# A layer kernel's state sums reordered: the second chunk's sum ahead of the state products, and VectorE's block layouts around gate times up

## The chip, the cores and the metric

The kernel runs on one core of one Trainium2 chip. The metric is device time in microseconds, the median of three runs. The span of a profiled execution is the time from its first instruction to its last. TensorE (PE in the profile) does the matrix products and is the only engine that writes PSUM here; VectorE (DVE), ScalarE (ACT) and GpSimd (POOL) work element by element; SyncE's queue (SP) issues the transfers.

## The reference

A normalised input goes through two branches that are added to the input: causal linear attention with 16 heads of 16 channels, and a mixture of four small gated MLPs with a router, plus a short convolution.

```python
x  = L0_attn_x                       # (8, 2048, 256) float32
xn = _layernorm(x)
# attention: q, k = relu(xn @ wq), relu(xn @ wk); v = xn @ wv
kv  = jnp.cumsum(k[..., :, None] * v[..., None, :], axis=2)
num = jnp.einsum('bhnd,bhnde->bhne', q, kv)
den = jnp.einsum('bhnd,bhnd->bhn', q, jnp.cumsum(k, axis=2))[..., None] + EPS
attn = (num / den) @ wo
# experts: top 2 of 8; four are MLPs, the others copies of x or relu(x), or nothing
g, u = jnp.einsum('th,ehi->tei', xn, Wg), jnp.einsum('th,ehi->tei', xn, Wu)
hid  = silu(g) * u
ffn  = sum_e cw_e * (hid_e @ Wd_e) + cw_4 * x + cw_6 * x + cw_7 * relu(x) + conv(x)
out  = x + attn + ffn
```

## The kernel before

The 8 sequences of 2048 tokens are cut into 32 batches of 512 tokens (`BT`), four to a sequence, and a batch into four tiles of 128 tokens (t = 0 to 3). A tile is two chunks of 64 tokens; chunk n = 2t + h. The causal sum is not formed for each token: within a chunk a masked score matrix (`sm`) times the values gives what the chunk's own tokens contribute, and a running 16x16 state for each head, summed over all earlier chunks, is multiplied with the queries.

All engines run their own programs, written out by hand, and meet at counting semaphores. One batch on TensorE (`batch`, in the section `block.tensor`) is, for each tile t:

- `gate_up(t)`: twelve products of 128x128 weights with 512 columns, for expert t (line 300 with `wgu_h` and `wgu_l`), six for the gate and six for up. Each half waits until VectorE has read the PSUM bank it writes: the gate half for `s_gu` (hid of the tile before), the up half for `s_y` (yT of the tile before).
- `numerators(t)`: `state_sum(2t + 1)` (line 371), then the scores times values (line 408), then the state times query (line 422), which ends with `s_num`, and then `state_sum(2t + 2)` except for the last tile.
- after tile 0 the next scores (line 357), after tile 1 the transposes of the next batch's input (line 310).

After the four tiles come the next batch's projections (`heads`) and the outputs of this batch (`output`).

`state_sum(n)` adds the keys-times-values product of chunk n to a running sum that stays in one PSUM bank (`ST`, "state_sum" in the profile). Before it may add, VectorE must have read the sum of the chunks before: it waits on `s_bd` for `blocks(n)`. VectorE's `blocks(n)` (line 760) waits on `s_st` for `state_sum(n - 1)`, multiplies the bank with a mask, and writes the block-diagonal operand `state_bd[:, n % 4]` that the state times query of chunk n uses. So the sums and the layouts form a chain that alternates between the engines: sum 2t+1, layout 2t+2, sum 2t+2, layout 2t+3.

On VectorE a tile is `gate_up(t)` (line 783: hid = up times silu of gate, waits for the up half and for ScalarE's silu), then `attend(t)`: layout 2t+2, the numerators over the denominators (yT, line 796), layout 2t+3. Then come two convolution taps (line 775), or after tile 0 the masking of the next scores (line 753). ScalarE and GpSimd split hid and yT into high and low parts for later products; GpSimd also weighs hid (line 626).

In the profile a float32 matmul appears as two passes, so that `state_sum`'s 8 products are 16 rows of a MATMUL, the 32 scores-times-values products 64, and the 8 state-times-query products 16. Their array shapes (rows by columns of weights) differ: 64x32 for `state_sum` and for scores times values, 128x64 for state times query, 128x128 for gate and up and for the transposes and projections, 32x64 for scores.

Of the kernel before, what the change touches and what calls it, by code (L numbers as in the profile page):

```python
# [15 lines left out]
def layer_kernel(nc, x, wqkv, wo, w_router, router_bias, w_gate, w_up, w_down, conv_w, conv_b,  # L16
# [6 lines left out]
    T = 4  # L23
    BT = T * P
    BPS = seq_len // BT
# [19 lines left out]
    with ExitStack() as ctx:  # L45
# [247 lines left out]
        def _(pe):  # L293
# [67 lines left out]
            def state_sum(s, j, k, n):  # L361

                first = (j + k) % BPS == 0 and n == 0
                if not first:
                    pe.wait_ge(s_bd, chunk_at(s, j + k, n))
                t, h = n // 2, n % 2
                toks = slice(h * HALF, (h + 1) * HALF)
                for g in range(C):
                    for m in range(PPG):
                        rows = slice(BLK * m, BLK * m + BLK)  # L370
                        ins = mm(ST[rows, g, :], ktok[toks, t, g, rows], vp[toks, t, g * PPG + m, 0:3:2, :],  # L371
                                 start=first and g == 0, stop=True, skip_group_check=True)
                ins.then_inc(s_st, 1)

            def batch(s, j, left):
                last = left == 0
                p = j % 2

                def gate_up(t):
                    for u in range(2):  # L380
                        if t == 0:

                            pe.wait_ge(s_out, at(s, j, T, 2 + u))
                        else:

                            pe.wait_ge((s_gu, s_y)[u], at(s, j, T, t))
                        product((GB, UB)[u][t % 2], [(wgu_h[:, u, t, c, :], wgu_l[:, u, t, c, :], xh[:, p, c, :],
                                                     xl[:, p, c, :]) for c in range(C)]
                                ).then_inc((s_gp, s_up)[u], 1)

                def numerators(t):
                    first_tile = j == 0 and t == 0
                    if t == 0:
                        pe.wait_ge(s_out, at(s, j, T, T))
                    pe.wait_ge(s_sg, at(s, j, T, t + 1))
                    if j < BPS - 1 or t < T - 1:
                        state_sum(s, j, 0, 2 * t + 1)
                    if t % 2 == 0:
                        pe.wait_ge(s_sm, at(s, j, U * ROWS, ROWS * (t // 2 + 1)))
                    for g in range(C):  # L400
                        gs = slice(g * HALF, (g + 1) * HALF)
                        for par in range(2):
                            for m in range(PPG):
                                pair = g * PPG + m
                                for h in range(2):
                                    toks = slice(h * HALF, (h + 1) * HALF)
                                    window = vp[toks, t, pair, par:par + 2, :].rearrange("p a d -> p (a d)")
                                    mm(NB2[t % 2][h][BLK * m:BLK * m + BLK, gs], window,  # L408
                                       sm[toks, t // 2, t % 2, 2 * pair + par, :], start=par == 0 and g == 0,
                                       stop=False, skip_group_check=True)  # L410
                    for h in range(2):
                        if first_tile and h == 0:
                            continue
                        n = 2 * t + h
                        pe.wait_ge(s_bd, chunk_at(s, j, n))
                        for g in range(C):
                            n0 = t * P + h * HALF
                            for w in range(2):

                                rows = slice(w * HALF, (w + 1) * HALF)  # L420
                                cols = slice(g * P + w * HALF, g * P + (w + 1) * HALF)
                                ins = mm(NB2[t % 2][h][rows, g * HALF:(g + 1) * HALF], state_bd[:, n % 4, cols],  # L422
                                         qT[:, g, n0:n0 + HALF], start=False, stop=True, skip_group_check=True)
                    ins.then_inc(s_num, 1)
                    if t < T - 1:
                        state_sum(s, j, 0, 2 * t + 2)

                def output(t):
                    ts = slice(t * P, (t + 1) * P)
                    dst = OB[t]  # L430
                    if t == 3:
                        pe.wait_ge(s_out, at(s, j, T, T + 1))
                    elif t == 0 or last:
                        pe.wait_ge((s_y, s_gu, s_y)[t], at(s, j, T, T))
                    else:
                        pe.wait_ge(s_sig, at(s, j, T, T + 2 + t))
                    if t == 0:
                        pe.wait_ge(s_conv, at(s, j, HALO, HALO))
                    for c in range(C):
                        mm(dst[:, c * P:(c + 1) * P], cT[:, c, ts], ident_s[:, :], is_transpose=True,  # L440
                           start=c == 0, stop=False, skip_group_check=True)
                    pe.wait_ge(s_yl, at(s, j, T, t + 1))
                    product(dst[:, 0:D], [(yh[:, c, ts], yl[:, c, ts], wo_h[:, c, :], wo_l[:, c, :])
                                          for c in range(C)], first=False, final=False)
                    for e in range(E):
                        if t == 0:
                            pe.wait_ge(s_hl, at(s, j, T, e + 1))
                        ins = product(dst[:, 0:D], [(hh[:, e, ts], hl[:, e, ts], wd_h[:, e, :], wd_l[:, e, :])],
                                      first=False, final=e == E - 1)
                    ins.then_inc(s_op, 1)  # L450

                for t in range(T):
                    gate_up(t)
                    numerators(t)
                    if t == 0:
                        scores(s, j, 0, 1)
                    if t == 1 and not last:
                        for c in range(C):
                            turn_xn(s, j, 1, c)
                if not last:  # L460
                    heads(s, j, 1)
                for t in range(T):
                    if t == T - 1 and not last:
                        scores(s, j, 1, 0)
                        state_sum(s, j, 1, 0)
                    output(t)
# [200 lines left out]
        def _(dve):  # L667
# [89 lines left out]
            def blocks(s, j, k, n):  # L757

                dve.wait_ge(s_st, chunk_at(s, j + k, n))
                dve.tensor_tensor(state_bd[:, n % 4, :].rearrange("p (g m n) -> p g m n", g=C, m=PPG),  # L760
                                  ST.unsqueeze(2).to_broadcast([P, C, PPG, BLK]),
                                  same_head_s[:, :].rearrange("p (m n) -> p m n", m=PPG).unsqueeze(1)
                                  .to_broadcast([P, C, PPG, BLK]), ALU.mult).then_inc(s_bd, 1)

            def batch(s, j, left):
# [17 lines left out]
                    dve.tensor_tensor(hid[:, t, :], UB[t % 2], sg[:, :], ALU.mult).then_inc(s_gu, 1)  # L783

                def attend(t):
                    if t < T - 1:
                        blocks(s, j, 0, 2 * t + 2)
                    elif j < BPS - 1:
                        blocks(s, j, 1, 0)
                    dve.wait_ge(s_num, at(s, j, T, t + 1))  # L790
                    if t > 1:
                        dve.wait_ge(s_yl, at(s, j, T, t - 1))
                    if t == 0:
                        dve.wait_ge(s_rd, at(s, j, C, C))
                    r = t % 2
                    dve.tensor_tensor(yT[:, t % 2, :, :].rearrange("p g (h n) -> p g h n", h=2),  # L796
                                      ring[:, r:r + 2, 0:P].rearrange("p h (g n) -> p g h n", g=C),
                                      rdT[:, :, t * P:(t + 1) * P].rearrange("p g (h n) -> p g h n", h=2),
                                      ALU.mult).then_inc(s_y, 1)
                    if t < T - 1:  # L800
                        blocks(s, j, 0, 2 * t + 3)

                for t in range(T):
                    gate_up(t)
                    attend(t)
                    if t == 0:
                        mask(s, j, 0, 1)
                    else:
                        tap(t)
# [92 lines left out]
```

## Time and profile before

| | |
|---|---|
| median of 3 runs | 1348.21 us (1348.19 to 1348.37) |
| the profiled execution's own time | 1346.54 us |
| its span | 1344.8 us |
| granted TensorE clock, mean | 0.997 of full speed |
| PE busy | 1313.8 us, 98% of the span |
| DVE busy | 1114.9 us, 83% |
| POOL / ACT busy | 814.9 us, 61% / 738.3 us, 55% |

Busy time counts an engine's instructions, not its waits. The matmul ends are modelled by the profiler, so 98% says that TensorE always had something in flight, and not that it ran at its peak. The chain that ended last is followed back from the last instruction; the engine that carries it is the one whose own instruction stream sets the time.

### The profile page before, as it was taken

What the parts mean: (1) busy time and instruction counts of PE and PEld (TensorE: products, weight loads), DVE (VectorE), ACT (ScalarE), POOL (GpSimd) and SP (SyncE); (2) the same over time, 40 slices, a digit from 0 to 9 for tenths busy, and PEclk for the clock granted to TensorE, in tenths of its full rate; (3) what the DMA queues carried; (4) which work ended last, traced back from release to release, by engine and by line L of the source; (5) the groups of instructions that cost most, each with busy time, mean ns of one, the idle gap of its engine ahead of it and who ended that gap; (6) DMA issues with size and microseconds to landing.
All of it is one profiled execution on the core that took longest, in us unless ns stands there. A gap on an engine that the chain in (4) does not pass through costs nothing.

```text
span 1344.8 us, 54748 instructions
## 1 busy us (share of the span) xinstructions
PE 1313.8 (98%) x24384; PEld 1136.4 (85%) x24384; DVE 1114.9 (83%) x2566; ACT 738.3 (55%) x1545; POOL 814.9 (61%) x679
## 2 busy tenths in 40 slices
PE   4899999999999999999999999999999999999997
PEld 3788888888888888888888888888888888888886
DVE  4888888888888888988888988888888889888885
ACT  4555665555664565654555655555645656545561
POOL 2755666755666656657556666556566566575554
PEclk9999999999999999999999999999999999999999
DMA  4011111111111211111111111121111111111110
GB/s 148 34 66 65 51 48 34 65 65 66 46 53 34 65 65 64 35 45 55 66 65 51 48 35 65 65 65 42 56 35 66 65 65 35 34 65 50 50 49 18
DMA packets 46779, 73.73 MB, mean 55 GB/s; under 512 B 6480, under 2 KB 42192, under 8 KB 42448
## 3 DMA queue, kind: packets, MB, share of 16 engines
q1 hardware_dynamic: 46544, 70.24, 15.1%
q8 instruction: 191, 3.13, 1.0%
q14 instruction: 44, 0.36, 0.1%
HBM read 53.18 MB, written 17.04 MB: 52 GB/s over the span
## 4 chain that ended last, share of the span: by engine, by line
PE 97%; DVE 1%; SPq 1%; ACT 1%; DMA 1%; issue 0%; DVEq 0%
PE ring L300 51%; PE scores L300 17%; PE ring L408 7%; PE ring L422 6%; PE scores L357 5%; PE state_sum L371 4%; PE ring L440 2%; PE scores L310 2%; PE scores L339 2%; DMA x_t<-in_L_attn_x_dram 1%; SPq L257 0%; DVE cT L775 0%; ACT qp L517 0%; DVE sm L753 0%; ACT xn L528 0%
## 5 line engine op out<-in xcount | busy, mean ns | idle before, releaser
L626 POOL TENSOR_TENSOR hid<-hid,cwb 128x512 f32<-128x512 f32 x128 | 169.8, 1327 | 202.6 <-DVE hid L783 200.8
L775 DVE SCALAR_TENSOR_TENSOR cT<-xT,conv_ws,cT 128x512 f32<-128x512 f32 x192 | 288.8, 1543 | 0.0
L614 POOL TENSOR_TENSOR x_t<-x_t,same 128x1024 f32<-128x1024 f32 x32 | 77.1, 2409 | 264.3 <-ACT same L524 264.3
L540 ACT ACTIVATE sg<-ring 128x512 f32<-128x512 f32 x128 | 76.7, 599 | 281.5 <-PE ring L300 281.5
L300 PE MATMUL ring<-xl,wgu_h 128*128 128x512 f32 x512 | 212.0, 414 | 0.0
L300 PE MATMUL ring<-xh,wgu_l 128*128 128x512 f32 x512 | 202.5, 396 | 0.0
L300 PE MATMUL ring<-xh,wgu_h 128*128 128x512 f32 x512 | 201.8, 394 | 0.0
L630 POOL TENSOR_TENSOR hl<-hid,hh 128x512 fp32r<-128x512 f32 x128 | 193.2, 1509 | 0.0
L783 DVE TENSOR_TENSOR hid<-ring,sg 128x512 f32<-128x512 f32 x128 | 88.2, 689 | 110.9 <-PE ring L300 110.9
L480 ACT ACTIVATE yh<-yT 128x256 fp32r<-128x256 f32 x128 | 53.5, 418 | 228.9 <-DVE yT L796 228.9
L753 DVE TENSOR_TENSOR sm<-scores,causal_s 128x512 f32<-128x512 f32 x256 | 158.7, 681 | 20.4 <-PE scores L357 20.2
L300 PE MATMUL ring<-wd_h,hl 128*128 128x256 f32 x512 | 143.7, 281 | 0.0
L300 PE MATMUL ring<-wd_h,hh 128*128 128x256 f32 x512 | 143.4, 280 | 0.0
L300 PE MATMUL ring<-wd_l,hh 128*128 128x256 f32 x512 | 143.2, 280 | 0.0
L635 POOL TENSOR_TENSOR yl<-yT,yh 128x256 fp32r<-128x256 f32 x128 | 132.7, 1036 | 7.7 <-ACT yh L480 7.2
L408 PE MATMUL ring<-sm,vp 64*32 64x64 f32 x8192 | 118.9, 225 | 0.0
L300 PEld LDWEIGHTS ring<-xl,wgu_h 128*128 128x128 f32 x512 | 96.8, 189 | 23.7 <-issue 5.5
L300 PEld LDWEIGHTS ring<-xh,wgu_l 128*128 128x128 f32 x512 | 96.4, 188 | 22.6
L300 PEld LDWEIGHTS ring<-xh,wgu_h 128*128 128x128 f32 x512 | 97.0, 190 | 17.3
L371 PEld LDWEIGHTS state_sum<-vp,ktok 64*32 64x32 f32 x3968 | 54.1, 107 | 57.8 <-issue 51.2
L760 DVE TENSOR_TENSOR state_bd<-state_sum,tables_s 128x256 f32<-128x256 f32 x248 | 102.6, 414 | 0.0
L408 PEld LDWEIGHTS ring<-sm,vp 64*32 64x32 f32 x8192 | 98.2, 105 | 2.9 <-issue 2.9
(110 smaller groups left out, 3542.6 us busy)
## 6 DMA issues: line engine op xcount, KB each, us to landing
cwb<-cw_rows SPq DMA_DIRECT2D x32, 1024.0 KB, 4.6
x_t<-in_L_attn_x_dram SPq DMA_DIRECT2D x32, 512.0 KB, 4.4
out_dram<-x_t SPq DMA_DIRECT2D x32, 512.0 KB, 2.9
cw_rows<-cwt SPq DMA_DIRECT2D x128, 2.0 KB, 1.4
sm<-in_L_attn_wqkv_dram SPq DMA_DIRECT2D x2, 384.0 KB, 5.5
sm<-in_L_ffn_Wg_dram SPq DMA_DIRECT2D x2, 256.0 KB, 4.2
sm<-in_L_ffn_Wu_dram SPq DMA_DIRECT2D x2, 256.0 KB, 5.8
cwb<-in_L_ffn_Wd_dram SPq DMA_DIRECT2D x1, 512.0 KB, 4.2
```

Source lines behind the costliest of these rows:

```text
L300: ins = mm(dst, lhs, rhs, start=first and n == 0, stop=final and n == len(passes) - 1, skip_group_check=not first)
L371: ins = mm(ST[rows, g, :], ktok[toks, t, g, rows], vp[toks, t, g * PPG + m, 0:3:2, :], start=first and g == 0, stop=True, skip_group_check ...
L408: mm(NB2[t % 2][h][BLK * m:BLK * m + BLK, gs], window, sm[toks, t // 2, t % 2, 2 * pair + par, :], start=par == 0 and g == 0, stop=False, ...
L422: ins = mm(NB2[t % 2][h][rows, g * HALF:(g + 1) * HALF], state_bd[:, n % 4, cols], qT[:, g, n0:n0 + HALF], start=False, stop=True, skip_gr ...
L614: pool.tensor_tensor(xb, xb, same[:, :, :], ALU.add).then_inc(s_base1, 1)
L626: pool.tensor_tensor(hid[:, e, :], hid[:, e, :], cwb[:, e, :], ALU.mult).then_inc(s_hid, 1)
L630: pool.tensor_tensor(hl[:, e, :], hid[:, e, :], hh[:, e, :].bitcast(F32), ALU.subtract).then_inc(s_hl, 1)
L635: pool.tensor_tensor(yl[:, :, t * P:(t + 1) * P], yT[:, t % 2, :, :], yh[:, :, t * P:(t + 1) * P].bitcast(F32), ALU.subtract).then_inc(s_y ...
L753: dve.tensor_tensor(heads, SB[f][:, :].rearrange("p (t a n) -> p t a n", a=2, n=HALF), causal2_s[:, :].unsqueeze(1).unsqueeze(1).to_broadc ...
L760: dve.tensor_tensor(state_bd[:, n % 4, :].rearrange("p (g m n) -> p g m n", g=C, m=PPG), ST.unsqueeze(2).to_broadcast([P, C, PPG, BLK]), s ...
L775: ins = dve.scalar_tensor_tensor(out=cT[:, c, :], in0=xT[:, j % 2, c, n:n + BT], scalar=conv_ws[:, c, n:n + 1], in1=cT[:, c, :], op0=ALU.m ...
L783: dve.tensor_tensor(hid[:, t, :], UB[t % 2], sg[:, :], ALU.mult).then_inc(s_gu, 1)
```

## The change

TensorE: the second state sum of a tile, `state_sum(2t + 2)`, is moved ahead of the state times query. VectorE: `blocks(2t + 2)` (for the last tile `blocks` of the next batch) is moved ahead of gate times up, and `blocks(2t + 3)` from behind yT to ahead of it.

```diff
@@ TensorE, numerators(t): after scores times values
+                    if t < T - 1:
+                        state_sum(s, j, 0, 2 * t + 2)
                     for h in range(2):
                         ...
                                 ins = mm(NB2[t % 2][h][rows, g * HALF:(g + 1) * HALF], state_bd[:, n % 4, cols],
                                          qT[:, g, n0:n0 + HALF], start=False, stop=True, skip_group_check=True)
                     ins.then_inc(s_num, 1)
-                    if t < T - 1:
-                        state_sum(s, j, 0, 2 * t + 2)
@@ VectorE
                 def attend(t):
-                    if t < T - 1:
-                        blocks(s, j, 0, 2 * t + 2)
-                    elif j < BPS - 1:
-                        blocks(s, j, 1, 0)
                     dve.wait_ge(s_num, at(s, j, T, t + 1))
                     ...
                                       ALU.mult).then_inc(s_y, 1)
+
+                for t in range(T):
+                    if t < T - 1:
+                        blocks(s, j, 0, 2 * t + 2)
+                    elif j < BPS - 1:
+                        blocks(s, j, 1, 0)
+                    gate_up(t)
                     if t < T - 1:
                         blocks(s, j, 0, 2 * t + 3)
-
-                for t in range(T):
-                    gate_up(t)
                     attend(t)
```

No instruction is added or removed. On TensorE, tile 1 of the first batch, before; `state_sum` is the running sum, `ring<-sm,vp` scores times values, `ring<-qT,state_bd` state times query:

```order
L371 MATMUL state_sum<-vp,ktok 32x32 [waits s_bd,s_sg]
L371 MATMUL state_sum<-vp,ktok 32x32 x7
L408 MATMUL ring<-sm,vp 32x64 x32
L422 MATMUL ring<-qT,state_bd 64x64 [waits s_bd]
L422 MATMUL ring<-qT,state_bd 64x64 x3
L422 MATMUL ring<-qT,state_bd 64x64 [waits s_bd]
L422 MATMUL ring<-qT,state_bd 64x64 x3
L371 MATMUL state_sum<-vp,ktok 32x32 [waits s_bd]
L371 MATMUL state_sum<-vp,ktok 32x32 x7
L310 MATMUL scores<-tables_s,xn 128x128 [waits s_sm,s_xn]
```

The same place in the changed kernel:

```order
L371 MATMUL state_sum<-vp,ktok 32x32 [waits s_bd,s_sg]
L371 MATMUL state_sum<-vp,ktok 32x32 x7
L408 MATMUL ring<-sm,vp 32x64 x32
L371 MATMUL state_sum<-vp,ktok 32x32 [waits s_bd]
L371 MATMUL state_sum<-vp,ktok 32x32 x7
L424 MATMUL ring<-qT,state_bd 64x64 [waits s_bd]
L424 MATMUL ring<-qT,state_bd 64x64 x3
L424 MATMUL ring<-qT,state_bd 64x64 [waits s_bd]
L424 MATMUL ring<-qT,state_bd 64x64 x3
L310 MATMUL scores<-tables_s,xn 128x128 [waits s_sm,s_xn]
```

The second sum stands right behind the products that have its array shape, and its wait for VectorE's layout now comes ahead of the state times query instead of behind it. On VectorE the same tile, before, from hid to the first tap:

```order
L783 TENSOR_TENSOR hid<-ring,sg 128x512 [waits s_up,s_sg]
L760 TENSOR_TENSOR state_bd<-state_sum,tables_s 128x256 [waits s_st]
L796 TENSOR_TENSOR yT<-ring,qks 128x256 [waits s_num]
L760 TENSOR_TENSOR state_bd<-state_sum,tables_s 128x256 [waits s_st]
L775 SCALAR_TENSOR_TENSOR cT<-xT,conv_ws,cT 128x512 [waits s_tap0]
```

And in the changed kernel:

```order
L760 TENSOR_TENSOR state_bd<-state_sum,tables_s 128x256 [waits s_st]
L783 TENSOR_TENSOR hid<-ring,sg 128x512 [waits s_up,s_sg]
L760 TENSOR_TENSOR state_bd<-state_sum,tables_s 128x256 [waits s_st]
L792 TENSOR_TENSOR yT<-ring,qks 128x256 [waits s_num]
L775 SCALAR_TENSOR_TENSOR cT<-xT,conv_ws,cT 128x512 [waits s_tap0]
```

Both layouts (L760) have moved one instruction forward: the first past hid, the second past yT. The TensorE move is made in the tiles 0, 1 and 2 of each of the 32 batches, 96 places; the VectorE move of the first layout also in tile 3, except in the last batch of a sequence.

## Rows read from the trace of the kernel before

**Rows 1.** The page: busy shares, and the chain that ended last.

```profile
PE 1313.8 (98%) x24384; PEld 1136.4 (85%) x24384; DVE 1114.9 (83%) x2566; ACT 738.3 (55%) x1545; POOL 814.9 (61%) x679
...
PE 97%; DVE 1%; SPq 1%; ACT 1%; DMA 1%; issue 0%; DVEq 0%
```

**Rows 2.** Waits of PE: who was waited for, us in total, times, longest.

```profile
PE scores L310 <- POOL xn L600: 10.0, 1, 10.0
PE scores L300 <- DVE wqk_l L833: 9.2, 1, 9.2
PE ring L440 <- DVE cT L775: 3.4, 1, 3.4
PE scores L357 <- ACT ktok L480: 2.3, 1, 2.3
PE state_sum L371 <- DVE state_bd L760: 2.2, 1, 2.2
```

**Rows 3.** Timeline of PE, a tile 2: start us, us, engine, line, op, out<-in.

```profile
626.04 0.40 PE L300 MATMUL ring<-xh,wgu_l 128*128 128x512 f32 x1
626.37 0.25 PE L371 MATMUL state_sum<-vp,ktok 64*32 64x32 f32 x5
...
626.50 0.19 PE L371 MATMUL state_sum<-vp,ktok 64*32 64x32 f32 x1
626.52 0.84 PE L408 MATMUL ring<-sm,vp 64*32 64x64 f32 x59
627.28 0.69 PE L422 MATMUL ring<-qT,state_bd 128*64 128x64 f32 x16
627.90 0.33 PE L371 MATMUL state_sum<-vp,ktok 64*32 64x32 f32 x16
628.16 0.51 PE L300 MATMUL ring<-xl,wgu_h 128*128 128x512 f32 x1
```

**Rows 4.** Durations of the lines 371, 422 and 760, min/median/max ns.

```profile
L371 PE MATMUL state_sum<-vp,ktok x3968: 186/193/260, 36.3 to 1321.9; 64*32 64x32 f32 x199
```

```profile
L422 PE MATMUL ring<-qT,state_bd x1984: 222/222/271, 44.0 to 1326.3; 128*64 128x64 f32 x199
```

```profile
L760 DVE TENSOR_TENSOR state_bd<-state_sum,tables_s x248: 405/415/425, 42.5 to 1322.2; 128x256 f32<-128x256 f32 x124
```

**Rows 5.** Timeline of PE, the tile 3 that follows.

```profile
632.05 0.69 PE L422 MATMUL ring<-qT,state_bd 128*64 128x64 f32 x16
632.67 0.39 PE L300 MATMUL scores<-wvr_l,xh 128*128 128x264 f32 x1
```

**Rows 6.** Timeline of DVE, the same tile 2.

```profile
626.55 0.69 DVE L783 TENSOR_TENSOR hid<-ring,sg 128x512 f32<-128x512 f32 x1 [0.62 <-PE ring L300]
627.15 0.41 DVE L760 TENSOR_TENSOR state_bd<-state_sum,tables_s 128x256 f32<-128x256 f32 x1
628.02 0.43 DVE L796 TENSOR_TENSOR yT<-ring,qks 128x256 f32<-128x256 f32 x1 [0.45 <-PE ring L422]
628.36 0.41 DVE L760 TENSOR_TENSOR state_bd<-state_sum,tables_s 128x256 f32<-128x256 f32 x1
628.69 2.45 DVE L775 SCALAR_TENSOR_TENSOR cT<-xT,conv_ws,cT 128x512 f32<-128x512 f32 x2
```

**Rows 7.** Timeline of PE and DVE, scores and their mask in a tile 0.

```profile
616.66 1.21 PE L357 MATMUL scores<-qp,kT 32*64 32x128 f32 x64
```

```profile
617.90 0.69 DVE L753 TENSOR_TENSOR sm<-scores,causal_s 128x512 f32<-128x512 f32 x1 [0.63 <-PE scores L357]
```

**Rows 8.** Timeline, PE restarted by DVE in the first tile.

```profile
42.55 0.41 DVE L760 TENSOR_TENSOR state_bd<-state_sum,tables_s 128x256 f32<-128x256 f32 x1
42.88 0.67 DVE L783 TENSOR_TENSOR hid<-ring,sg 128x512 f32<-128x512 f32 x1
43.07 0.18 PEld L371 LDWEIGHTS state_sum<-vp,ktok 64*32 64x32 f32 x9 [2.58 <-issue]
43.10 0.25 PE L371 MATMUL state_sum<-vp,ktok 64*32 64x32 f32 x7 [2.17 <-DVE state_bd L760]
```

**Rows 9.** Timeline, the first projection restarted by DVE.

```profile
19.77 1.28 DVE L833 TENSOR_TENSOR wqk_l<-sm,wqk_h 128x512 fp32r<-128x512 f32 x2
...
21.11 0.59 PE L300 MATMUL scores<-wvr_l,xh 128*128 128x264 f32 x1 [9.19 <-DVE wqk_l L833]
```

**Rows 10.** Groups of GpSimd: busy us, mean ns, idle before and its releaser.

```profile
L626 POOL TENSOR_TENSOR hid<-hid,cwb 128x512 f32<-128x512 f32 x128 | 169.8, 1327 | 202.6 <-DVE hid L783 200.8
L635 POOL TENSOR_TENSOR yl<-yT,yh 128x256 fp32r<-128x256 f32 x128 | 132.7, 1036 | 7.7 <-ACT yh L480 7.2
```

## The prediction

> **What bounds the kernel now.** I read the page first: its busy shares put PE at 98% and DVE at 83%, and the chain that ended last is 97% PE [rows 1]. The list of PE's waits then says where PE was held up: five places, once each, 27.1 us together, four of them before the first tile's numerators are over and one at the end [rows 2]. In the steady state of 32 batches PE never waits for anyone. The time is therefore the length of PE's own instruction stream, and an edit counts by what it does to the spacing of PE's instructions, or by a wait that it puts where there was none. Spacing is read from starts in the timeline, since the ends are modelled.
>
> A tile of PE's stream in starts [rows 3]: last up product 626.04, first state sum 626.37 to 626.50, scores times values until about 627.14 (the 59 merged rows end at 627.36, and I take one to last 0.22, as the matmuls of state times query with the same 64 columns do [rows 4]), state times query at 627.28, second state sum at 627.90, next gate product at 628.16. Two kinds of boundary can be seen. Between the first sum and scores times values, both on 64x32 weights, there is no gap: the first scores row falls among the sum's. Where the array shape changes there is one: 627.14 to 627.28 is 0.14. The state times query lasts 0.62 from its first start to the first start of what follows, whether that is the state sum (627.28 to 627.90) or a 128x128 product (632.05 to 632.67) [rows 3, 5]. The second sum lasts 0.26 to the next shape.
>
> **The change on TensorE, without a wait.** The stream from the last scores row to the next gate product is now 0.14 + 0.62 + 0.26 = 1.02. With the second sum first there is nothing to switch ahead of it: about 0.01 + 0.26 + 0.62 = 0.89. That is 0.13 less in each of 96 places, 12.5 us in all. This needs that the switch from the sum to state times query costs what its switch to 128x128 does; the pair with the same two shapes, from scores times values to state times query, has 0.14 for 64 columns, so the price is in the right place.
>
> The Trainium skill, page TensorEngine Tiling (Array Packing), section Key Properties, says that changing the tiling mode, not merely the tile, drains TensorE. The 0.14 at the change of shape against none within a shape [rows 3] agrees with it, and by this rule alone the change is a gain of one drain for each place. It says nothing of what the drain hid.
>
> **The wait that takes its place.** The second sum needs layout 2t+2, and that needs the first sum. Before, state times query lay between: the layout ran from 627.15 to 627.56 and the second sum started at 627.90, so the wait was always over [rows 3, 6]. Now only scores times values is in between. Step by step, in the clock of rows 3:
>
> - The last row of the first sum ends at 626.50 + 0.19 = 626.69.
> - VectorE starts after it by a lag. Behind the scores, streams of 128 columns, it is 617.90 - 617.87 = 0.03; behind state times query, 64 columns, 628.02 - 627.97 = 0.05 [rows 3, 6, 7]. The shorter the stream, the later the true end behind the modelled one. For 32 columns I take 0.07, with 0.03 and 0.09 as the ends. VectorE is free: it stood idle for 0.62 before 626.55. The layout starts at 626.76.
> - The layout takes 0.415 [rows 4]: done at 627.175.
> - PE restarts. The only state sum that ever waited for a layout started at 43.10 after a layout that ended at 42.96: 0.14 [rows 8]. The nearest other value is the first projection, 21.11 after an end of 21.05: 0.06 [rows 9]. I take 0.14, from the same two instructions. The second sum starts at 627.315.
> - Then 0.26 for the sum and 0.62 for state times query: the next product starts at 628.195, against 628.16 now.
>
> So each place becomes about 0.04 longer, and not 0.13 shorter: the wait, 627.315 against 627.15, costs 0.17 and swallows the switch that is saved. 96 x 0.04 = 3.8 us. The ends: lag 0.03 and restart 0.06 give 628.075, -0.085 a place, -8 us; lag 0.09, restart 0.14 and a switch of 0.05 more into state times query, because its weights could not be loaded while PE stood waiting, give +0.11, +10 us.
>
> **The change on VectorE.** hid of the tile starts behind the layout. The next instruction of VectorE starts 0.33 after a layout (42.55 to 42.88 [rows 8]), so hid goes from 626.55 to 627.09 and ends at 627.78 instead of 627.24. What waits for it: in tile 2 the next gate product directly, due at 628.195; with a restart of 0.14 it may start at 627.92, so 0.28 is left (in tiles 0 and 1 scores or transposes stand between as well). GpSimd's weighing waits for hid, 200.8 us in all, but nothing downstream of it is waited for by PE [rows 2, 10]. yT waits for the end of state times query, which starts at 627.315 + 0.26 = 627.575 instead of 627.28: yT goes from 628.02 to 628.32 and ends at 628.75. The next up product, six products of some 0.23 behind 628.2, is due near 629.6, so 0.85 is left. Behind yT the second layout is gone, so the taps start at 628.32 + 0.34 = 628.66 against 628.69: VectorE's day is as long as before. In tile 3 VectorE alone changes; yT there still waits for the state times query and PE's stream is the same. At the end of the program PE waits for the taps once (3.4 us [rows 2]); these move by no more than the stream. All this I cost at nothing.
>
> The sum: the profiled execution, 1346.54, would take 1350.3. The median of the runs is 1.67 above the profiled one, so the same 3.8 us on the median give 1348.21 + 3.8 = 1352.0.
>
> **Rivals.**
>
> 1. The wait is mostly hidden and the saved switch remains (faster). The mechanism is PE's restart: if it takes 0.06 as in rows 9, with the lag at 0.07, the next product starts at 628.115, -0.045 a place, -4.3 us: 1343.9. With no wait at all it is the full 0.13, 1335.7. For it: the drain is visible and is really removed. Against it: rows 8 are the very pair, a layout and a state sum, and the layout alone ends at 627.175, later than the last scores row. It decides below a restart of 0.10. The skill's rule on modes gives the 1335.7. Chance 0.15, of which the full gain has little.
> 2. The two cancel closer than I can read (no change). 0.04 is the difference of 0.17 and 0.13, each known to 0.02 or 0.03. Within 0.028 a place, 2.7 us or 0.2%, which is about what a measurement of this kernel can tell from no change, it is the same: some 1349.5. For it: the rows have two decimals and the lag is extrapolated; with a lag of 0.05 the difference is 0.02. Chance 0.27.
> 3. The stall costs more than its own length (slower by more). Behind a wait PE starts with nothing loaded: if one load of the 128x64 weights comes to stand in the open, 0.07 to 0.14 a place, the time is 1359 to 1365. Against it: after the one wait of this kind the sum's rows follow each other within hundredths [rows 8]. Or hid becomes late for the gate product: it must slip by more than 0.28, and tile 2 is only 32 places. Chance 0.08.
> 4. The change does not do what it says, for PE may already take the second sum's weights early. The rows show the second sum's first start 0.62 after state times query begins, the same as another shape, so nothing is taken early; no chance of its own.
>
> The Trainium skill, page TensorE: Matmul & The Clock Gate, Part 3, says that TensorE can pull a weight load ahead of matmuls in flight when it does not conflict. Behind an unmet wait that help is gone, which is what rival 3 would make of it; no row here shows its price.
>
> **How the numbers follow.** The forecast, 1352.0 with its own range of 1351 to 1356, has 0.50; rival 1 0.15, rival 2 0.27, rival 3 0.08. The likeliest is the 1352.0. Slower by over 0.2% is the forecast and rival 3, 0.58; within 0.2% is rival 2, 0.27; faster 0.15. The range for 8 in 10 leaves out the full gain and the dearest stall: 1344.5 to 1357.
>
> **What would show it.** In the changed profile the waits of PE gain a row of the state sum waiting for the layout, some 95 times at about 0.15, 12 to 17 us together. The timeline of a tile should read, from the last up product: first layout at +0.72, last scores row at +1.10, second sum at +1.27, state times query at +1.53, next product at +2.15 (now 2.12). hid starts half a microsecond later. PE's busy time falls by about the wait. It would prove me wrong if the second sum's row is not waiting, if the gap from it to state times query is not 0.12 to 0.14, or if waits of PE for hid or yT appear.

## The result, and the profile after

The changed kernel is faster, by a third of a per cent:

| | before | after |
|---|---|---|
| median of 12 runs each | 1348.05 us | 1342.91 us |
| ratio, 95% interval | | 0.9965 [0.9954, 0.9976] |
| profiled execution, its own time | 1346.54 us | 1342.80 us |
| its span | 1344.8 us | 1341.0 us |

The ratio is 4.7 us (3.2 to 6.2) on 1348. The forecast was 1352.0, slower, and its range ended at 1344.5.

The page, busy shares and chain, answers to [rows 1]:

```profile
PE 1310.1 (98%) x24384; PEld 1136.4 (85%) x24384; DVE 1116.7 (83%) x2566; ACT 739.3 (55%) x1545; POOL 826.3 (62%) x679
...
PE 97%; DVE 1%; SPq 1%; ACT 1%; DMA 1%; issue 0%; DVEq 0%
```

PE is still the chain, and its busy time fell by 3.7 us while the span fell by 3.8. PE's list of waits, against [rows 2]:

```profile
PE scores L310 <- POOL xn L600: 10.0, 1, 10.0
PE scores L300 <- DVE wqk_l L833: 9.3, 1, 9.3
PE ring L440 <- DVE cT L775: 3.1, 1, 3.1
PE scores L357 <- ACT ktok L480: 2.3, 1, 2.3
PE state_sum L371 <- DVE state_bd L760: 2.2, 1, 2.2
```

No wait has appeared there. That doesn't say that there is none. The timeline of PE in a tile 2, against [rows 3] (start us, us, engine, line, op, out<-in), shows where it hides:

```profile
583.72 0.40 PE L300 MATMUL ring<-xh,wgu_l 128*128 128x512 f32 x1
...
584.13 0.21 PE L371 MATMUL state_sum<-vp,ktok 64*32 64x32 f32 x3
...
584.19 0.84 PE L408 MATMUL ring<-sm,vp 64*32 64x64 f32 x59
584.92 0.33 PE L371 MATMUL state_sum<-vp,ktok 64*32 64x32 f32 x16
585.18 0.69 PE L424 MATMUL ring<-qT,state_bd 128*64 128x64 f32 x16
585.79 0.50 PE L300 MATMUL ring<-xl,wgu_h 128*128 128x512 f32 x1
```

The 59 rows of scores times values end, as modelled, at 585.03, so the last of them, which takes 0.22, started at 584.81. The second sum starts at 584.92, 0.11 later, where its rows should follow at 0.01 to 0.02. The modelled end of the row before lies behind 584.92 and covers the standstill; only the starts show it. The tile runs from 583.72 to 585.79, 2.07 us, against 626.04 to 628.16, 2.12 [rows 3]. Over the 96 places the spans differ by 3.8 us, 0.04 each; the rows have two decimals.

VectorE in the same tile, against [rows 6]:

```profile
584.44 0.42 DVE L760 TENSOR_TENSOR state_bd<-state_sum,tables_s 128x256 f32<-128x256 f32 x1 [0.93 <-PE state_sum L371]
584.78 0.68 DVE L783 TENSOR_TENSOR hid<-ring,sg 128x512 f32<-128x512 f32 x1
585.38 0.42 DVE L760 TENSOR_TENSOR state_bd<-state_sum,tables_s 128x256 f32<-128x256 f32 x1
585.91 0.42 DVE L792 TENSOR_TENSOR yT<-ring,qks 128x256 f32<-128x256 f32 x1
```

The layout ends at 584.86 and the second sum starts at 584.92: PE restarted 0.06 after it. In [rows 8] the same pair of instructions took 0.14, and the prediction had built on that. So the question for the experiments is why one restart takes 0.14 and the other 0.06. The other row that the prediction had, [rows 9], also took 0.06. VectorE's idle time now stands ahead of the layout, and PE's first sum is what ends it:

```profile
L760 DVE TENSOR_TENSOR state_bd<-state_sum,tables_s 128x256 f32<-128x256 f32 x248 | 103.7, 418 | 136.1 <-PE state_sum L371 136.1
```

### The profile page after: what moved, and what is told of

Same layout as the page of the kernel before. It is cut to its first block, busy times and chain, and to the rows that moved or that the text cites. A ratio compares the mean times of both kernels' runs of the same rounds, so it can differ in the third digit from the quotient of the medians.

```text
span 1341.0 us, 54748 instructions
## 1 busy us (share of the span) xinstructions
PE 1310.1 (98%) x24384; PEld 1136.4 (85%) x24384; DVE 1116.7 (83%) x2566; ACT 739.3 (55%) x1545; POOL 826.3 (62%) x679
## 4 chain that ended last, share of the span: by engine, by line
PE 97%; DVE 1%; SPq 1%; ACT 1%; DMA 1%; issue 0%; DVEq 0%
PE ring L300 51%; PE scores L300 17%; PE ring L408 7%; PE ring L424 6%; PE scores L357 5%; PE state_sum L371 4%; PE ring L440 2%; PE scores L310 2%; PE scores L339 2%; DMA x_t<-in_L_attn_x_dram 1%; SPq L257 0%; DVE cT L775 0%; DVE sm L753 0%; ACT qp L517 0%; ACT xn L528 0%
## 5 line engine op out<-in xcount | busy, mean ns | idle before, releaser
L775 DVE SCALAR_TENSOR_TENSOR cT<-xT,conv_ws,cT 128x512 f32<-128x512 f32 x192 | 292.9, 1564 | 0.0
L760 DVE TENSOR_TENSOR state_bd<-state_sum,tables_s 128x256 f32<-128x256 f32 x248 | 103.7, 418 | 136.1 <-PE state_sum L371 136.1
L630 POOL TENSOR_TENSOR hl<-hid,hh 128x512 fp32r<-128x512 f32 x128 | 208.1, 1626 | 0.0
L300 PE MATMUL scores<-xh,wqk_l 128*128 128x512 f32 x256 | 100.2, 392 | 0.0
```

The costliest lines, as they stand in the source:

```text
L300: ins = mm(dst, lhs, rhs, start=first and n == 0, stop=final and n == len(passes) - 1, skip_group_check=not first)
L630: pool.tensor_tensor(hl[:, e, :], hid[:, e, :], hh[:, e, :].bitcast(F32), ALU.subtract).then_inc(s_hl, 1)
L775: ins = dve.scalar_tensor_tensor(out=cT[:, c, :], in0=xT[:, j % 2, c, n:n + BT], scalar=conv_ws[:, c, n:n + 1], in1=cT[:, c, :], op0=ALU.m ...
```

## The experiments

The theories. A: a restart depends on where the blocking wait stands among the waits of its instruction. The first sum of the first tile has three waits written one behind another (`s_out`, `s_sg`, and last `s_bd`, the one that blocks), the second sum of a tile has `s_bd` alone. B: it depends on how long PE had stood still, over 2 us in the first tile and 0.1 in the second sum. C: the number of waits counts, wherever the blocking one stands. The kernel before already has a row on this, and I had not read it so: the first projection [rows 9] stands behind three waits too (`w_split`, `s_xh`, `s_xl`), but the one for VectorE's low weight parts (`w_split`), which blocks, is written first. It restarted 0.06 after VectorE's end, after PE had stood still for 9.19 us. That is what A says, and neither B nor C. It is one row of another pair of instructions, so the runs below have to decide. Apart from that I wanted the worth of the saved change of shape by itself, and the change in its two halves. Ratios are against runs of the kernel before on the same chip.

**TensorE's half alone.** In the kernel before:

```diff
@@ TensorE, numerators(t)
+                    if t < T - 1:
+                        state_sum(s, j, 0, 2 * t + 2)
                     for h in range(2):
                         ...
                     ins.then_inc(s_num, 1)
-                    if t < T - 1:
-                        state_sum(s, j, 0, 2 * t + 2)
```

> TensorE's half of the change alone: the second sum stands ahead of state times query, VectorE is in the order of before, so that layout 2t+2 comes behind hid (start 1.11 us after the last up product, done at 1.53). Both theories: PE now waits for it until about 1.59, state times query at 1.84, next product at 2.47 instead of 2.12; 96 places of 0.35 us, 33 us slower than before: 1381. The wait is some 0.48 us long at a place, five times that of the changed kernel. Theory A (PE's restart depends on where the blocking wait stands among the waits of its instruction, and this one is the only one): the restart from the layout's end stays near 0.06. Theory B (the restart depends on how long PE had stood still): it moves towards 0.14, which adds up to 8 us: 1389.

Measured: 1380.49 us, ratio 1.0240 [1.0220, 1.0261], 32 us slower. The wait is now long enough to show in PE's list:

```profile
PE state_sum L371 <- DVE state_bd L760: 27.8, 96, 2.2
```

In a tile 2, VectorE's hid and layout, and PE:

```profile
601.35 0.69 DVE L783 TENSOR_TENSOR hid<-ring,sg 128x512 f32<-128x512 f32 x1 [0.97 <-PE ring L300]
601.96 0.41 DVE L760 TENSOR_TENSOR state_bd<-state_sum,tables_s 128x256 f32<-128x256 f32 x1
```

```profile
602.43 0.33 PE L371 MATMUL state_sum<-vp,ktok 64*32 64x32 f32 x16 [0.27 <-DVE state_bd L760]
```

The layout ends at 602.37, PE starts at 602.43: 0.06 again, after a standstill some five times as long as in the changed kernel. That speaks against B. It also shows what VectorE's half is for: without it the moved sum costs 32 us, since its layout stands behind hid.

**VectorE's half alone.** The change with TensorE's order of before:

```diff
@@ TensorE, numerators(t)
-                    if t < T - 1:
-                        state_sum(s, j, 0, 2 * t + 2)
                     for h in range(2):
                         ...
                     ins.then_inc(s_num, 1)
+                    if t < T - 1:
+                        state_sum(s, j, 0, 2 * t + 2)
```

> VectorE's half of the change alone: the layouts ahead of hid and of yT, TensorE in the order of before (second sum behind state times query). yT now stands behind layout 2t+3, which waits for the late second sum: yT starts at about 2.60 us after the last up product instead of 1.98, and ends at 3.03. Theory: TensorE's next up product is due at 3.5, so it waits for nothing and the time is that of before, within 2 us of 1348; the whole gain comes from TensorE's order. Rival (earlier layouts help by themselves): 1345 or less. Rival (late yT or hid reaches TensorE through GpSimd): over 1351, with waits of PE in the list.

Measured: 1346.65 us against 1346.59, ratio 0.9995 [0.9985, 1.0006]. No change, as the theory had it. yT stands behind a layout that waits for the late second sum, and PE does not notice:

```profile
588.51 0.42 DVE L760 TENSOR_TENSOR state_bd<-state_sum,tables_s 128x256 f32<-128x256 f32 x1 [0.51 <-PE state_sum L371]
588.85 0.41 DVE L792 TENSOR_TENSOR yT<-ring,qks 128x256 f32<-128x256 f32 x1
```

This tile's last up product was at 586.25, so yT is at +2.60 where [rows 6] has +1.98.

**A second wait ahead of the blocking one.** In the changed kernel:

```diff
@@ TensorE, numerators(t)
                     if t < T - 1:
+                        pe.wait_ge(s_sg, at(s, j, T, t + 1))
                         state_sum(s, j, 0, 2 * t + 2)
```

> The changed kernel with a second wait at the second sum, written ahead of the wait for the layout, on a semaphore (silu's) that has long reached its value. Theory A (a blocking wait that is written behind another wait restarts PE later): the second sum starts 0.08 us later, at 1.285 after the last up product, in each of 96 places: 8 us slower than the changed kernel, about 1351, which is what the prediction had. Theory B (length of the standstill): nothing changes, 1343. Theory C (the number of waits alone counts): 1351 here and in the next kernel as well.

**The same wait behind the blocking one.** In the changed kernel:

```diff
@@ TensorE, state_sum(s, j, k, n)
                 if not first:
                     pe.wait_ge(s_bd, chunk_at(s, j + k, n))
+                if k == 0 and n % 2 == 0:
+                    pe.wait_ge(s_sg, at(s, j, T, n // 2))
```

> The same second wait, written behind the wait for the layout. Theory A: nothing changes against the changed kernel, 1343, the second sum stays at 1.205 after the last up product. Theory B: 1343 as well. Theory C (number of waits): 1351.

Measured, together: with the wait ahead 1350.93 us, ratio 1.0026 [1.0015, 1.0036]; with it behind 1342.91 us, ratio 0.9964 [0.9950, 0.9978], that of the changed kernel. The two differ in the order of two lines, and by 8 us, 0.083 a place. With the wait ahead, layout and second sum in a tile 2:

```profile
588.59 0.43 DVE L761 TENSOR_TENSOR state_bd<-state_sum,tables_s 128x256 f32<-128x256 f32 x1 [1.03 <-PE state_sum L371]
```

```profile
589.16 0.33 PE L371 MATMUL state_sum<-vp,ktok 64*32 64x32 f32 x16
```

From 589.02 to 589.16, 0.14. With it behind:

```profile
585.16 0.43 DVE L762 TENSOR_TENSOR state_bd<-state_sum,tables_s 128x256 f32<-128x256 f32 x1 [0.94 <-PE state_sum L373]
```

```profile
585.64 0.33 PE L373 MATMUL state_sum<-vp,ktok 64*32 64x32 f32 x16
```

From 585.59 to 585.64, 0.05. The traces also show what the order does. Where an instruction of TensorE has several waits, a separate semaphore instruction stands ahead of it (PEldq is TensorE's sequencer). By lines of kernel.py, with the wait ahead, and with it behind:

```profile
L365 PEldq EVENT_SEMAPHORE  x216: 51/51/1917, 41.9 to 1327.2; - x108
```

```profile
L365 PEldq EVENT_SEMAPHORE  x120: 51/51/1914, 43.1 to 1315.6; - x120
L367 PEldq EVENT_SEMAPHORE  x96: 51/51/51, 43.8 to 1318.7; - x96
```

In both kernels line 365 is the wait for the layout; line 367 of the second is the added wait. The 120 are those of the first sums, as in the changed kernel. The 96 of the second sums are at the layout's wait where it is written second, and at the added wait where that is. So the wait that is written later becomes the separate instruction, which takes 51 ns even when it waits for nothing, and the one written first stays with the weight load and the matmul. In the two tiles above: with the wait ahead, the separate instruction runs from 589.05 to 589.10, behind the layout's end at 589.02, the weight load starts at 589.13 and the matmul at 589.16. With it behind, the separate instruction starts at 585.44, before the layout's end at 585.59, and load and matmul start together at 585.64. B and C fall: the standstill and the number of waits are about the same in the two, and only the order differs. An additional wait that is already over costs nothing if it is written behind the blocking one.

**One wait after a long standstill.** The other side of it, in the changed kernel: the first sum keeps its layout's wait alone.

```diff
@@ TensorE, numerators(t)
-                    if t == 0:
-                        pe.wait_ge(s_out, at(s, j, T, T))
-                    pe.wait_ge(s_sg, at(s, j, T, t + 1))
                     if j < BPS - 1 or t < T - 1:
                         state_sum(s, j, 0, 2 * t + 1)
+                    if t == 0:
+                        pe.wait_ge(s_out, at(s, j, T, T))
+                    pe.wait_ge(s_sg, at(s, j, T, t + 1))
```

> The changed kernel with the waits for silu (and in tile 0 for the stored output) moved from ahead of the first sum to behind it, so that the first sum of the first tile waits for its layout alone, after TensorE has stood still for over 2 us. Theory A (place of the blocking wait among several): TensorE restarts 0.05 us after the layout's end instead of 0.14. Theory B (length of the standstill): 0.14 as before. The time stays at 1343 by both.

This is a single run, and its time (1345.78 us) decides nothing: the 17 runs of before on its chip lie between 1344.26 and 1350.20 us. Its rows of the first tile answer to [rows 8]:

```profile
41.22 0.41 DVE L760 TENSOR_TENSOR state_bd<-state_sum,tables_s 128x256 f32<-128x256 f32 x1
41.68 0.22 PEld L371 LDWEIGHTS state_sum<-vp,ktok 64*32 64x32 f32 x16 [2.44 <-DVE state_bd L760]
41.68 0.33 PE L371 MATMUL state_sum<-vp,ktok 64*32 64x32 f32 x16 [2.00 <-DVE state_bd L760]
```

The layout ends at 41.63 and PE starts at 41.68, 0.05, after it had stood still for 2 us, where the changed kernel with its three waits has 0.15 in the same place:

```profile
42.42 0.41 DVE L760 TENSOR_TENSOR state_bd<-state_sum,tables_s 128x256 f32<-128x256 f32 x1
42.95 0.18 PEld L371 LDWEIGHTS state_sum<-vp,ktok 64*32 64x32 f32 x9 [2.57 <-issue]
42.98 0.25 PE L371 MATMUL state_sum<-vp,ktok 64*32 64x32 f32 x7 [2.17 <-DVE state_bd L760]
```

So theory A holds in both directions, for long and short standstills. With one wait there is no separate semaphore instruction left at line 365 in this trace, and weight load and matmul start together (41.68); with three the load starts at 42.95, 0.12 after the layout's end, and the matmul 0.03 behind it.

The Trainium skill, page Perfetto Trace Analysis, section Identifying Dependency Chains, says that an instruction that waits for several engines may have separate semaphore instructions, with the additional waits, put ahead of it. The rows at the lines 365 and 367 agree. The price of 0.08 to 0.09 us and the order are this case's measurement.

**The saved change of shape without the wait.** In the changed kernel:

```diff
@@ TensorE, state_sum(s, j, k, n); ST2 is a part of scores bank 3
                 first = (j + k) % BPS == 0 and n == 0
-                if not first:
+                apart = k == 0 and n > 0 and n % 2 == 0
+                if apart:
+                    pe.wait_ge(s_sm, at(s, j, U * ROWS, ROWS * (1 if n == 2 else 2)))
+                elif not first:
                     pe.wait_ge(s_bd, chunk_at(s, j + k, n))
...
-                        ins = mm(ST[rows, g, :], ktok[toks, t, g, rows], ...
-                                 start=first and g == 0, ...
+                        ins = mm((ST2 if apart else ST)[rows, g, :], ktok[toks, t, g, rows], ...
+                                 start=(first or apart) and g == 0, ...
```

> The changed kernel with the second sum of a tile written to another PSUM bank that nothing reads (a free bank of the scores), so that it need not wait for layout 2t+2. The second sums are then missing from the state, and the output is not the reference's. It shows what the saved change of array shape is worth without the wait. Theory: the second sum starts at 1.11 after the last up product, state times query at 1.37, the next product at 1.98 instead of 2.12 before: 96 x 0.135 = 13 us below before, 1335. Rival (the gap of 0.14 ahead of state times query in the kernel before is a wait or the pipeline's own, not the shape): the gap only moves, and it stays within 3 us of the changed kernel, 1340 to 1343.

The wait for `s_sm` in the cut makes sure that the scores in that bank have been read; it adds no standstill in the rows below. Measured: 1331.80 us, ratio 0.9879 [0.9863, 0.9894], 16 us below before (14 to 18). In a tile 2:

```profile
582.35 0.40 PE L301 MATMUL ring<-xh,wgu_l 128*128 128x512 f32 x1
...
582.82 0.78 PE L412 MATMUL ring<-sm,vp 64*32 64x64 f32 x55
...
583.45 0.32 PE L375 MATMUL scores<-vp,ktok 64*32 64x32 f32 x13
583.70 0.69 PE L428 MATMUL ring<-qT,state_bd 128*64 128x64 f32 x16
584.31 0.50 PE L301 MATMUL ring<-xl,wgu_h 128*128 128x512 f32 x1
```

1.96 from the last up product to the next product, about 0.15 less than before (2.12) and 0.11 less than with the change (2.07). The rival falls: the gap was the change of shape and it goes when the shape doesn't change. It is a little more than the 0.13 that I had, because the sum's rows also begin among the last ones of scores times values, as the first sum's do (the merged rows break off at 55 of 59, and 13 of the sum's 16 are left). The remaining wait of the changed kernel is thus worth some 11 us.

**A version that releases the sum earlier.** The second sum has to wait until PSUM was read, not until the layout is built. VectorE copies the 64 columns and builds the layout from the copy, behind hid (with `copied=True`, `blocks` waits for the copy and reads it in place of the bank):

```diff
@@ TensorE, state_sum
-                if not first:
+                if k == 0 and n > 0 and n % 2 == 0:
+                    pe.wait_ge(s_cp, at(s, j, T - 1, n // 2))
+                elif not first:
                     pe.wait_ge(s_bd, chunk_at(s, j + k, n))
@@ VectorE
+            def copy_sum(s, j, n):
+                dve.wait_ge(s_st, chunk_at(s, j, n))
+                dve.tensor_scalar(stc[:, :, :], ST, 1.0, None, ALU.mult).then_inc(s_cp, 1)
...
                     if t < T - 1:
-                        blocks(s, j, 0, 2 * t + 2)
+                        copy_sum(s, j, 2 * t + 2)
                     ...
                     gate_up(t)
                     if t < T - 1:
+                        blocks(s, j, 0, 2 * t + 2, copied=True)
                         blocks(s, j, 0, 2 * t + 3)
```

> A version meant to be faster. VectorE first copies the running sum out of PSUM (128x64 elements), which releases the second sum, and builds layout 2t+2 from the copy behind hid; the rest is the changed kernel. Theory: the copy starts at 0.73 us after the last up product and takes 0.2 or so against 0.42 for the layout, so that it is done near 0.95, before the last row of scores times values at 1.10: no wait is left, the next product is at about 1.97, and the time is that of the kernel whose second sum did not wait, 1332 (1330 to 1335). VectorE gets 96 more instructions but stays off the path. Rival (VectorE's added work, or yT behind two layouts, becomes late for TensorE): waits of PE for VectorE appear and the time is 1338 or more. Rival (the last kernel gained through its other bank and not through the missing wait): 1340 or more.

Measured: 1333.17 us against 1346.59 before on its chip, ratio 0.9902 [0.9887, 0.9917]. It is 13 us (11 to 15) faster than before and beats the changed kernel's 0.9965; the intervals don't touch. In a tile 2:

```profile
578.10 0.40 PE L302 MATMUL ring<-xh,wgu_l 128*128 128x512 f32 x1
...
580.07 0.51 PE L302 MATMUL ring<-xl,wgu_h 128*128 128x512 f32 x1
```

```profile
578.82 0.23 DVE L763 TENSOR_SCALAR stc<-state_sum 128x64 f32<-128x64 f32 x1 [0.92 <-PE state_sum L375]
578.97 0.68 DVE L794 TENSOR_TENSOR hid<-ring,sg 128x512 f32<-128x512 f32 x1
579.56 1.34 DVE L771 TENSOR_TENSOR state_bd<-stc,tables_s 128x256 f32<-128x256 f32 x1
```

The copy ends at 579.05, +0.95, before the last row of scores times values (+1.10), and the tile takes 1.97 as the one without a wait. PE's list of waits has no new row. Both rivals of this run fall.

## Why the prediction was wrong, step by step

- **PE's stream bounds the kernel.** Right: the span fell by 3.8 us and PE's busy time by 3.7, and VectorE's half alone moved nothing.
- **The saved change of shape, 0.13 a place.** Right in kind, a little small: about 0.15 in the run without a wait.
- **The lag and the layout.** Right: predicted start at +0.72 after the last up product, measured 584.44 - 583.72 = +0.72; predicted 0.415, measured 0.42.
- **"PE restarts. [...] I take 0.14, from the same two instructions."** This step failed. It is 0.06, and with that the sum gives rival 1's 1343.9, where 1342.9 was measured. The 0.08 a place too much is 8 us over 96 places, and it turned -4 into +4. The one row was the very pair of instructions, but not with the same waits: the order of before prints `[waits s_bd,s_sg]` at the first sum and `[waits s_bd]` at the second, and stood in the section on the change. The two kernels that differ only in the order of two waits show that this order decides. The row at 0.06 [rows 9], which the prediction set aside as another pair, had its blocking wait first and was the one to take.
- **The unblocked rest.** Right: the sum lasts 0.26 to the next shape (584.92 to 585.18) and state times query 0.61 (585.18 to 585.79); I had 0.26 and 0.62. No weight load came into the open behind the wait; rival 3 has nothing for it.
- **VectorE's costs at nothing.** Right: hid at +1.06 (predicted 627.09 - 626.04 = 1.05), yT at +2.19 (predicted +2.28, with the 0.08 of the failed step in it), and no wait of PE for either appears. Even yT at +2.60, with VectorE's half alone, costs nothing.
- **What would show it.** Besides the starts that hang on the failed step (next product at +2.07, not +2.15), wrong in one thing: I expected a row in PE's waits, and PE's busy time to fall by the wait. A wait shorter than the modelled length of the matmul ahead of it is counted as busy time; it has to be read from the starts. For the same reason "PE never waits for anyone" could not be read from that list for waits as short as this.
- **The chances.** The failed step had been named as rival 1's mechanism, with the right price, and given 0.15, because a single row of the same pair seemed to outweigh the other one. Two rows that disagree by 0.08 on a step that is paid 96 times should have kept both signs nearly equal, and their waits in kernel.py would have told which to use.

## What to carry to other kernels

Where TensorE waits on several semaphores ahead of one instruction, write the wait that blocks first, and take a restart's price only from a row whose waits have the same number and order. On an engine that is the bound, keep instructions of one array shape together, and ask of each wait what exactly it waits for: here it was the read of PSUM, which is a part of the operation only, and copying first took the gain from 5 to 13 us. A wait of a tenth of a microsecond doesn't appear in the list of waits of TensorE; look at the starts.

## What the runs showed of the hardware

- PE's restart after VectorE's end: 0.05 to 0.06 us with the blocking wait alone or written first, 0.14 to 0.15 with it written behind another. The short one was seen after standstills of 0.1, 0.5, 2 and 9 us, the long one after 0.2 and 2 us. The later-written wait is a separate instruction of 51 ns at least.
- At a change of array shape, from the last start before it to the first behind it: 0.12 behind a state sum (changed kernel: last of its rows at 584.92 + 0.33 - 0.19 = 585.06, state times query at 585.18), 0.14 to 0.15 behind the products with 64 columns. Within one shape the next group's rows begin among the last ones (the 55 of 59 rows above).
- A layout from the copy in SBUF takes longer at times than one from PSUM (405 to 425 ns [rows 4]): 416 ns at the median, but 1344 at most:

```profile
L771 DVE TENSOR_TENSOR state_bd<-stc,tables_s x96: 414/416/1344, 42.1 to 1308.1; 128x256 f32<-128x256 f32 x96
```

In the long one shown above (579.56 to 580.90) GpSimd was in an SBUF operation from 578.47 to 580.61. What holds VectorE up there was not tested. It is off the path here; it would not be if the second sum waited for it.
